# Graph attention behind a graph ODE on one Trainium2 core: transposed probabilities leave PSUM tile by tile instead of pair by pair, and the value product runs two rows at a time

## What is computed

```python
h = jnp.maximum(_layernorm(x, axis=-1), 0.0)
x = x + _L0_gnn_ref(h, adj, ...)
h = jnp.maximum(_layernorm(x, axis=-1), 0.0)
# second layer, for each of the 16 batches, N = 512, H = 4, HEAD_DIM = 32
qkv = h @ W
mask = jnp.where(adj == 0, -jnp.inf, 0.0)
scores = jnp.einsum('bhid,bhjd->bhij', q, k) / np.sqrt(HEAD_DIM) + mask
attn = jax.nn.softmax(scores, axis=-1)
out = jnp.einsum('bhij,bhjd->bhid', attn, v)
x = x + out
```

## Time and profile before

| | us |
|---|---|
| median of 3 runs (lowest, highest) | 734.52 (733.99, 735.31) |
| span of the profiled execution | 730.3 |
| TensorE busy | 692.7 (95%) |
| VectorE busy | 486.1 (67%) |
| ScalarE busy | 400.9 (55%) |
| GpSimd busy | 121.2 (17%) |

### The profile page before, as it was taken

How to read it: one execution, slowest core, us unless ns; L and a number is a source line. 1 busy time by engine, 2 the same in 40 slices (tenths; PEclk the granted TensorE clock), 3 DMA queues, 4 the chain that set the end, 5 groups by cost and what they waited for, 6 DMA issues and landing times. The chain is left out here.

```text
span 730.3 us, 12946 instructions
## 1 busy us (share of the span) xinstructions
PE 692.7 (95%) x3801; PEld 517.3 (71%) x3801; DVE 486.1 (67%) x1272; ACT 400.9 (55%) x860; POOL 121.2 (17%) x100
## 2 busy tenths in 40 slices
PE   7999999998999989999998779999999999999996
PEld 5768987898888978899887655565655555566553
DVE  6753552578337873466346578888888888888883
ACT  3442231233522444222334678888888888888883
POOL 4110343032401233012315000000000000000001
PEclk8999999999999999999998999999999999999999
DMA  3001110311342124400449892666676766766620
GB/s 104 30 0 44 30 44 0 101 31 44 145 167 78 57 80 162 132 15 16 158 175 256 287 213 74 152 139 150 155 158 158 158 148 154 158 157 152 153 57 29
DMA packets 49807, 82.52 MB, mean 113 GB/s; under 512 B 5232, under 2 KB 13808, under 8 KB 49648
## 3 DMA queue, kind: packets, MB, share of 16 engines
q1 hardware_dynamic: 49344, 82.07, 42.5%
q10 hardware_dynamic: 432, 0.07, 0.1%
HBM read 52.76 MB, written 29.36 MB: 112 GB/s over the span
## 5 line engine op out<-in xcount | busy, mean ns | idle before, releaser
L1292 DVE CUSTOM_DVE_ANT_0 s_ring<-ps_s,pL 128x512 f32<-128x512 f32 x256 | 169.0, 688 | 55.0 <-PE ps_s L1334 53.1
L1269 ACT ACTIVATE s_ring<-s_ring,low 128x512 f32<-128x512 f32 x256 | 182.2, 713 | 16.3 <-DVE low L1292 14.8
L1321 PE MATMUL ps_t<-ident,s_ring 128*128 128x128 f32 x1024 | 155.7, 275 | 9.6 <-DVE p_t L1286 9.0
L1321 PEld LDWEIGHTS ps_t<-ident,s_ring 128*128 128x128 f32 x1024 | 127.0, 141 | 31.5 <-DVE p_t L1286 11.6
L1334 PE MATMUL ps_s<-pL,pH 128*128 128x512 f32 x256 | 126.0, 495 | 6.9 <-DMA pL<-qk_dram 3.7
L1334 PEld LDWEIGHTS ps_s<-pL,pH 128*128 128x128 f32 x256 | 48.9, 192 | 75.5 <-DVE low L1292 56.6
L1349 PE MATMUL ps_o<-p_t,v_sb 128*32 128x512 f32 x512 | 95.6, 603 | 1.1 <-ACT p_t L1260 1.1
L1286 DVE COPY p_t<-ps_t 128x1024 f32<-128x1024 f32 x64 | 78.1, 1220 | 0.0
L1260 ACT ACTIVATE p_t<-ps_t 128x1024 f32<-128x1024 f32 x64 | 64.9, 1014 | 21.3 <-PE ps_t L1321 21.3
L1246 POOL TENSOR_TENSOR o_n<-o_n,x 128x512 f32<-128x512 f32 x16 | 20.6, 1285 | 311.4 <-DVE o_n L1302 311.4
L94 PE MATMUL ps_v<-rH,ut_h 128*128 128x384 f32 x192 | 65.1, 339 | 4.6 <-DVE v L927 4.6
(11 more groups left out here) (201 smaller groups left out, 1087.3 us busy)
## 6 DMA issues: line engine op xcount, KB each, us to landing
pH<-qk_dram SPq DMA_DIRECT2D x64, 256.0 KB, 7.6
pL<-qk_dram SPq DMA_DIRECT2D x64, 256.0 KB, 8.4
qk_dram<-qk SPq DMA_DIRECT2D x12, 512.0 KB, 3.3
x_ln<-in_x SPq DMA_DIRECT2D x16, 256.0 KB, 3.3
x_res<-in_x SPq DMA_DIRECT2D x16, 256.0 KB, 2.6
x_dram<-v SPq DMA_DIRECT2D x16, 256.0 KB, 3.1
v_sb<-v_dram SPq DMA_DIRECT2D x16, 256.0 KB, 2.7
x<-x_dram SPq DMA_DIRECT2D x16, 256.0 KB, 2.9
```

Of the source, the lines that this page charges most:

```text
L1269: act.activation(s_ring[:, n % RING, :], s_ring[:, n % RING, :], ACT.Exp, bias=low[:, n:n + 1], scale=-1.0, accum_out=lsum[par][:, n:n + 1 ...
L1292: dve.tensor_tensor_reduce(s_ring[:, n % RING, :], ps_s[S_BANK[n]][:, :], mask[:, n // HEADS, :], -SCALE, 3.0e38, ALU.add, ALU.min, low[:, ...
L1321: mm = pe.transpose(ps_t[p % 2][:, n % 2, j * 128:(j + 1) * 128], s_ring[:, n % RING, j * 128:(j + 1) * 128], ident[:, :])
```

## The change

Four things change together, all in `attention_block`:

- `ps_t` becomes a ring of four single banks instead of two pairs of banks. Tile n goes through bank n % 4, and T(n) waits for the copy of tile n - 4.
- Each copy takes one tile, one bank and 512 columns: 16 copies per batch instead of 8. `COPIER` gives eight to VectorE (tiles 0, 1, 3, 5, 7, 8, 12, 14) and eight to ScalarE (2, 4, 6, 9, 10, 11, 13, 15). `COPY_AT` is the slot ahead of which a copy stands: 7, 7, 8, 9, 9, 12, 11, 15, 15, 15, 16, 17, 19, 18, 21, 20 for tiles 0 to 15. Below: C(n).
- `LAG` is 5 instead of 4.
- The value product stands in slots 7 and 14, eight matmuls (two rows) in each, instead of in five slots with 1, 4, 2, 4 and 5. The copy of `ps_o` stands ahead of E(14) instead of E(13).

```diff
--- before.py
+++ after.py
@@ -1113,18 +1113,23 @@
         return ctx.enter_context(nc.semaphore(name))
 
     TILES = T * HEADS
-    PAIRS = TILES // 2
     RING = 8
-    LAG = 4
-    ACT_PAIRS = [1, 2, 5, 7]
-    DVE_PAIRS = [p for p in range(PAIRS) if p not in ACT_PAIRS]
-
-    COPY_BEFORE = [7, 7, 8, 12, 14, 15, 18, 18]
-
-
-    PV_AT = {5: 1, 6: 4, 7: 2, 11: 4, 13: 5}
-    OCOPY_AT, OT_AT, FIN_AT = 13, 15, 15
-    assert sum(PV_AT.values()) == HEADS * T
+    LAG = 5
+    T_BANKS = 4
+    COPIER = "DDADADADDAAADADA"
+    ACT_TILES = [n for n in range(TILES) if COPIER[n] == "A"]
+    DVE_TILES = [n for n in range(TILES) if COPIER[n] == "D"]
+
+    COPY_AFTER = [2, 1, 1, 1, 0, 2, 0, 3, 2, 1, 1, 1, 2, 0, 2, 0]
+    COPY_AT = [n + LAG + after for n, after in enumerate(COPY_AFTER)]
+    for mine in (ACT_TILES, DVE_TILES):
+        order = [COPY_AT[n] for n in mine]
+        assert order == sorted(order) and order[-1] - TILES < order[0]
+
+
+    PV_AT = {7: 8, 14: 8}
+    OCOPY_AT, OT_AT, FIN_AT = 14, 15, 15
+    assert sum(PV_AT.values()) == HEADS * T and all(n % HEADS == 0 for n in PV_AT.values())
     PV_RANGE = [(sum(PV_AT.get(i, 0) for i in range(n)), sum(PV_AT.get(i, 0) for i in range(n + 1))) for n in range(TILES)]
 
     S_BANKS = 3
@@ -1145,7 +1150,7 @@
     x1 = [sb(f"x1_{i}", [128, T * D]) for i in range(2)]
 
     ps_s = [ctx.enter_context(nc.psum_tensor(f"ps_s{i}", [128, N], F32)) for i in range(S_BANKS)]
-    ps_t = [ctx.enter_context(nc.psum_tensor(f"ps_t{i}", [128, 2, N], F32)) for i in range(2)]
+    ps_t = [ctx.enter_context(nc.psum_tensor(f"ps_t{i}", [128, N], F32)) for i in range(T_BANKS)]
     ps_o = ctx.enter_context(nc.psum_tensor("ps_o", [128, N], F32))
     ps_n = ps_o
 
@@ -1173,23 +1178,23 @@
         batch(B - 1, (B - 1) % 2)
         tail(B, B % 2)
 
-    def copied(p, b):
-
-        if p in ACT_PAIRS:
-            return t_act, len(ACT_PAIRS) * b + ACT_PAIRS.index(p) + 1
-        return t_dve, len(DVE_PAIRS) * b + DVE_PAIRS.index(p) + 1
-
-    def pairs_before(n, mine):
-
-        return [(p, COPY_BEFORE[p] // TILES) for p in mine if COPY_BEFORE[p] % TILES == n]
-
-    def copy_pair(eng, p, b, par):
-        wait(eng, t_mm, TILES * b + 2 * p + 2)
-        if p in (ACT_PAIRS[0], DVE_PAIRS[0]):
+    def copied(n, b):
+
+        if n in ACT_TILES:
+            return t_act, len(ACT_TILES) * b + ACT_TILES.index(n) + 1
+        return t_dve, len(DVE_TILES) * b + DVE_TILES.index(n) + 1
+
+    def tiles_before(n, mine):
+
+        return [(m, COPY_AT[m] // TILES) for m in mine if COPY_AT[m] % TILES == n]
+
+    def copy_tile(eng, m, b, par):
+        wait(eng, t_mm, TILES * b + m + 1)
+        if m in (ACT_TILES[0], DVE_TILES[0]):
             wait(eng, pv_mm, CREDIT + b - 1)
-        it, h = divmod(2 * p, HEADS)
-        dst = p_t[par][:, h:h + 2, :, it * 128:(it + 1) * 128]
-        src = ps_t[p % 2][:, :, :].rearrange("p h (j i) -> p h j i", j=T)
+        it, h = divmod(m, HEADS)
+        dst = p_t[par][:, h, :, it * 128:(it + 1) * 128]
+        src = ps_t[m % T_BANKS][:, :].rearrange("p (j i) -> p j i", j=T)
         return dst, src
 
     block = ctx.enter_context(nc.Block())
@@ -1253,10 +1258,10 @@
         def batch(b, par, tiles=TILES):
             first = isinstance(b, int) and b == 0
             for n in range(TILES):
-                for p, back in pairs_before(n, ACT_PAIRS):
+                for m, back in tiles_before(n, ACT_TILES):
                     if (first and back) or not (tiles or back):
                         continue
-                    dst, src = copy_pair(act, p, b - back, (par + back) % 2)
+                    dst, src = copy_tile(act, m, b - back, (par + back) % 2)
                     act.activation(dst, src, ACT.Copy).then_inc(t_act, 1)
                 if n == OCOPY_AT and not first:
                     wait(act, pv_mm, CREDIT + b)
@@ -1279,10 +1284,10 @@
         def batch(b, par, tiles=TILES):
             first = isinstance(b, int) and b == 0
             for n in range(TILES):
-                for p, back in pairs_before(n, DVE_PAIRS):
+                for m, back in tiles_before(n, DVE_TILES):
                     if (first and back) or not (tiles or back):
                         continue
-                    dst, src = copy_pair(dve, p, b - back, (par + back) % 2)
+                    dst, src = copy_tile(dve, m, b - back, (par + back) % 2)
                     dve.tensor_copy(dst, src).then_inc(t_dve, 1)
                 if tiles:
                     wait(dve, s_mm, CREDIT + TILES * b + n + 1)
@@ -1311,14 +1316,12 @@
     def _(pe):
         def transposes(n, b):
 
-            p = n // 2
             wait(pe, p_done, TILES * b + n + 1)
-            if n % 2 == 0:
-                s, value = copied(p - 2, b) if p >= 2 else copied(p - 2 + PAIRS, b - 1)
-                if not (isinstance(b, int) and b == 0 and p < 2):
-                    wait(pe, s, value)
+            s, value = copied(n - T_BANKS, b) if n >= T_BANKS else copied(n - T_BANKS + TILES, b - 1)
+            if not (isinstance(b, int) and b == 0 and n < T_BANKS):
+                wait(pe, s, value)
             for j in range(T):
-                mm = pe.transpose(ps_t[p % 2][:, n % 2, j * 128:(j + 1) * 128],
+                mm = pe.transpose(ps_t[n % T_BANKS][:, j * 128:(j + 1) * 128],
                                   s_ring[:, n % RING, j * 128:(j + 1) * 128], ident[:, :])
             mm.then_inc(t_mm, 1)
 
@@ -1341,8 +1344,8 @@
 
                     j, hh = divmod(k, HEADS)
                     if k == 0:
-                        for p in (ACT_PAIRS[-1], DVE_PAIRS[-1]):
-                            wait(pe, *copied(p, c))
+                        for m in (ACT_TILES[-1], DVE_TILES[-1]):
+                            wait(pe, *copied(m, c))
                         wait(pe, v_in[cp], parity_count(c, cp, 16))
                         wait(pe, o_div, CREDIT + c)
                     cols = slice(HD * hh, HD * (hh + 1))
```

## The result

The changed kernel takes 708.04 us (median of 4 runs, 704.25 to 710.90) against 734.91 us (median of 4, 733.99 to 736.56): the ratio is 0.9631, 95% interval 0.9601 to 0.9662. It is 27 us faster; the forecast was 38, and 697 us. Its runs also lie further apart than those of before.

The account below looks back on a forecast made before the run. TensorE bound the kernel, busy 18.5 of 19.1 us a batch; at 16.6 us a batch, 15 x 2.48 plus 0.4 saves 37.6 us, so the 730.3 us span becomes 692.7, plus 4.2 makes 697 us; range 689 to 715.

Parts of the forecast that it names:

- The value product: On TensorE, two runs of eight matmuls at 1.83 us plus 0.21 each replace five runs, saving 2.7 us a batch.
- The walk through three engines: Hand-over path of one batch through ScalarE, TensorE and VectorE: 16.5 to 16.6 us with half the loop's turn.
- both of its waits: VectorE waits for scores ahead of mask M(8), 0.5 us, and ahead of mask M(15), 0.2 to 0.4 us.
- The copies: Single-tile copies of 512 columns should show about 0.69 us on VectorE and 0.60 on ScalarE.
- the case that is slower: Rival: TensorE idles in pieces, its clock falls, six slow slots make a batch 20.2 us, 751 us in all; chance 0.06.
- The loads as a second limit: Loads for batch b + 2 leave at b's end, so two batches take at least 15.6 + 17.4 = 33.0 us.
- The tail: After the last batch, the last copy takes 0.60 us instead of 1.02, saving 0.4 us.
- nothing is gained there: Batch 0 has no value product and batch 1's first score waits for a load, so neither gains time.
- The ring: Four single banks with lag five let transposes wait for an earlier copy, saving 1.0 us a batch on TensorE.
- The 1.0 us stall goes: TensorE's transposes no longer wait for VectorE's 1.15 us copy of a pair, about 1.0 us a batch.
- The loads bind: Rival: v's load holds back q and k by 1.1 us, a batch is 17.3 us, 707 us; chance 0.10.
- the last rival: The eight matmuls of a value product run do not overlap across heads, so a run costs more; chance 0.02.

Follow-up runs that it names:

- early loads: Changed kernel with the q and k loads for batch b + 2 moved ahead of the residual's load and the store, waiting only for batch b's last score matmul: 698.1 us.

## Why the prediction was right in direction and 11 us off

**Right.** *The value product:* a run of 16 records takes 1.85 to 1.92 us, forecast 1.83, and this term is the gain. *The walk through three engines:* 16.56 us a batch where nothing else binds, forecast 16.5 to 16.6, with both of its waits at their places. *The copies:* 0.685 and 0.583 us. *The clock:* 1.00 in the steady batches, so the case that is slower did not come. (What the Trainium skill tells of a kernel that cycles through PSUM banks, TensorE: Matmul & The Clock Gate, section A second HAM failure mode, this trace does not show: TensorE idles in several pieces in each batch and keeps its clock.) *The loads as a second limit,* and its form: two batches cannot be shorter than from the first score to the o_t transposes, plus from these to the landing.

**The step that failed** is the size of one term, the time from the o_t transposes to the landing of q and k, 17.4 us in the limit of the loads: "The last q and k bytes land at about 581.3, where the DMA share falls off, 17.2 us behind the o_t transposes". The DMA share does end there. What the score waits for is the semaphore that the load raises when it has landed, and the profile has its time too, in the answer for the line's last loads (the very last is issued at 572.36, in the kernel before):

```profile
DMA to landing us min/median/max: 9.0/9.4/9.8
```

That is at most 9.8 us, so 582.16: 0.9 us later than I read, and 18.0 behind the transposes. For the batch before it the same reading is 563.43, or 18.5. The kernel before had 0.9 and 1.1 us to spare ahead of those two first scores, not the 2.2 that the prediction gave. (The Trainium skill, DMA: Bandwidth & Descriptors, section Anatomy of one DMA, which follows a DMA from GpSimd, says why a reader should expect this: the semaphore cannot be raised until the last byte is confirmed as landed. The trace agrees in kind; in the two batches it shows 0.7 to 0.9 us from the end of the last stretch with busy DMA engines to the landing.) In the changed kernel the term is 18.3 (539.87 to 558.20, by the timeline, which has the start of these transposes 0.16 us earlier than the chain has). Read the same way, its mean over the loads for batches 4 to 15 is 18.3 us in both kernels: the change left this path as it was, and the forecast had read it some 0.8 us too short. The first part is 15.54 (524.33 to 539.87), for which the walk had 15.6. Half their sum is 16.9 where the forecast had 16.5; from batch 4 on the mean distance is 17.1. With both limits at 16.5 the prediction let them stand side by side at 16.6; in truth one stood half a microsecond above the other, and with it the hand-over's waits were free.

Beside it there is one long wait, which no term of the forecast has: the loads for batch 3 landed 16.2 us after the first was issued instead of 13.3 to 14.6 (the sixth was held 1.42 us in its issue). The chain there, the first score's row, and the clock behind it:

```profile
460.70 11.60 DMA pL<-qk_dram
...
472.42 0.49 PE ps_s L1337
```

```profile
472.40:476.00 3.60, 3.58 (x16) 3.09 (x16) 1.70 (x5) 2.04 (x5) 0.00 (x0) 0.57 0.72 183
```

That batch distance was 20.31 us, 3.2 more than the others. Why that issue was held was not tried, and whether every execution has this wait is not known.

*Where the 11 us lie,* in the profiled execution. From batch 1's first score to batch 15's it took 243.5 us, where the forecast had 14 x 16.6 = 232.4: 11.1 us, some 5 of them from the term above and 3.2 from the long wait. The tail came out as forecast. There is also a loss at the start that the prediction put at nothing ("nothing is gained there"): batch 1's first score came at 434.53 instead of 430.19, 4.3 us later, since attention began 2.1 us later and the loads that this score waits for took 16.4 us from the first issue instead of 14.3. Whether that belongs to the change is open: in the runs of the experiments this score comes anywhere from 430.4 to 434.0. What makes up for it is the 2.4 us below, and 1.5 us by which the profiled execution is slower than the median.

*The ring* was priced at 1.0 us a batch. Alone it was worth nothing, and beside the product and early loads 0.4. The step "The 1.0 us stall goes" is true of that stall, 0.57 us of idle time and the slower matmuls behind it, and wrong as a gain: the next waits on the same list, for C(11) and C(15), were about as long.

*The rivals.* "The loads bind" was given 0.10 and 707 us, and is what happened; its reason, the load of v getting in the way, is not, as the run with a quarter of v showed; so its number is near by luck. (Slower should have had 0.07, the clock's 0.06 and half of the last rival's 0.02, and the prediction gave 0.06.) *Outside the span* lie 1.75 us (709.55 for the profiled execution that spans 707.8), not the 4.2 that I took; the other 2.4 are the kernel before's own spread, between its profiled execution and its median.

## What to carry to other kernels

A limit that lies close under the one you remove deserves the most careful reading of all: here a prefetch had 1 us to spare, and the change needed 2.5. Read the end of a transfer from its landing, the time at which the waiting engine may go on, and not from where the DMA engines fall idle; then ask what releases its issue, because a load that waits in a queue behind the end of the last batch makes a loop over two batches that faster engines do not shorten. When several small edits come together, run each alone, but put its work where its inputs are ready: moving one run of the value product by one slot cost this kernel 17 us, and moving its five runs by one or two slots 45 us, more than the whole change gained.

## What the runs showed of the hardware

- The semaphore of a 256 KB load came some 0.7 to 0.9 us after the DMA share had fallen to nothing: 582.16 against a last busy stretch that ends by 581.5, and 563.43 against 562.5.
- Eight loads of 256 KB from one queue, behind each other, land 13.8 us after the first is issued, on average, in both kernels.
- After TensorE stood still for 3.7 us its granted clock was 0.57 over the next 3.6 us; after waits of up to 1.93 us (at 593.14 and 628.02) it stayed 1.00.
- Matmuls of one row of the value product overlap across four column positions, and the time of a run goes with the number of rows that it begins: 0.98 us for one matmul, 0.99 for four, 1.92 for eight, 3.64 for sixteen.
